# A bilinear tap's corner 3 scaled on ScalarE and added on VectorE in one instruction, with two buffers for its turned values

## The reference

```python
def _L0_conv_ref(x, ...):
    out = relu(frozen_bn(conv2d(x, w1), ...))                 # 1x1, 1024 -> 256
    offset = conv2d(out, w_off, pad=1, bias=b_off)            # 3x3, 256 -> 18
    out = deform_conv3x3(out, offset, w2, pad=1, dil=1)       # 256 -> 256
    out = relu(frozen_bn(out, ...))
    out = frozen_bn(conv2d(out, w3), ...)                     # 1x1, 256 -> 1024
    return relu(out + x)

# inside deform_conv3x3, for each of 9 taps and each pixel, at a position (py, px):
val = (gather(y0, x0) * (wy0 * wx0) + gather(y0, x1) * (wy0 * wx1)
       + gather(y1, x0) * (wy1 * wx0) + gather(y1, x1) * (wy1 * wx1))
return einsum('nckhw,ock->nohw', val, w)

def _L1_conv_ref(x, mask, w1, w2, w3):
    out = relu(_gconv(x * m1, w1, 0)) * m2                    # 4 groups, 1024 -> 256
    out = relu(_gconv(out, w2, 1)) * m2                       # 4 groups, 3x3
    return relu(_gconv(out, w3, 0) + residual)                # 256 -> 1024
```

## Time and profile before

| | |
|---|---|
| median of 3 runs | 2840.26 us (2840.18 to 2841.08) |
| the profiled execution | 2831.85 us |
| its span | 2830.1 us |
| TensorE busy | 2749.0 us, 97% |
| VectorE busy | 2276.2 us, 80% |
| ScalarE busy | 1225.2 us, 43% |
| POOL busy | 1241.1 us, 44% |

### The profile page before, as it was taken

The page is one execution under the profiler, slowest core; times in us unless marked ns, Lnnn a source line. Parts: engine busy times, 40 slices in busy tenths (PEclk is TensorE's granted clock), DMA queues, the critical chain, the costliest instruction groups (busy, mean ns, idle before and its releaser), DMA issues.

```text
span 2830.1 us, 39439 instructions
## 1 busy us (share of the span) xinstructions
PE 2749.0 (97%) x12960; PEld 1518.7 (54%) x12960; DVE 2276.2 (80%) x5216; ACT 1225.2 (43%) x2466; POOL 1241.1 (44%) x1159
## 2 busy tenths in 40 slices
PE   8969999999999999999999999999999999999998
PEld 3435555555555555555555555555555555555552
DVE  2148888888888888888888888888889888888871
ACT  1124444444444444444444444444444444444442
POOL 2046544444444444444444444444444555555530
PEclk9989999999999999999999999999999999999999
DMA  8679988889888899888889988889988888888861
GB/s 328 227 278 343 328 304 303 325 325 333 305 312 298 321 331 328 313 314 303 306 326 325 332 305 309 299 326 327 332 306 295 303 316 317 314 317 318 316 230 77
DMA packets 263691, 864.38 MB, mean 305 GB/s; under 512 B 31810, under 2 KB 72898, under 8 KB 255168
## 3 DMA queue, kind: packets, MB, share of 16 engines
q0 software_dynamic: 165888, 604.05, 60.0%
q1 hardware_dynamic: 79168, 190.68, 18.7%
q10 hardware_dynamic: 18432, 67.12, 6.0%
HBM read 747.72 MB, written 114.02 MB: 304 GB/s over the span
## 4 chain that ended last, share of the span: by engine, by line
PE 93%; DVE 4%; issue 1%; DMA 1%; ACT 1%; SPq 0%; POOL 0%; DVEq 0%; POOLq 0%; ACTq 0%
PE psR L529 15%; PE psA L416 15%; PE psD L509 9%; PE psV L490 9%; PE psD L510 9%; PE psD L511 9%; PE psR L563 9%; PE psR L580 5%; PE psR L542 4%; PE psA L457 3%; PE psR L586 3%; DVE val L947 2%; DVE y L930 1%; PE psD L457 1%; PE psA L437 1%
## 5 line engine op out<-in xcount | busy, mean ns | idle before, releaser
L379 POOL DMA_INDIRECT corners<-corner_tables,samples_in x1152 | 1226.2, 1064 | 1489.1 <-DVE val L947 1056.8
L947 DVE SCALAR_TENSOR_TENSOR val<-corners,samples_in,val 128x256 f32<-128x256 f32 x3456 | 1417.3, 478 | 30.0 <-ACT val L697 24.6
L711 ACT ACTIVATE valT_hi<-psV 128x512 fp32r<-128x512 f32 x576 | 311.6, 593 | 912.8 <-PE psD L511 691.9
L957 DVE TENSOR_TENSOR valT_lo<-psV,valT_hi 128x512 fp32r<-128x512 f32 x576 | 370.5, 685 | 239.0 <-ACT valT_hi L711 222.2
L697 ACT ACTIVATE val<-corners,samples_in 128x256 f32<-128x256 f32 x1152 | 490.4, 503 | 32.9 <-DMA corners<-corner_tables,samples_in 29.1
L509 PE MATMUL psD<-valT_hi,w_hi 128*128 128x512 f32 x1152 | 483.4, 420 | 0.4 <-DVE valT_lo L957 0.4
L529 PE MATMUL psR<-deformed,w_sb 128*128 128x512 f32 x1024 | 463.3, 595 | 2.4 <-ACT y L739 1.9
L510 PE MATMUL psD<-valT_hi,w_lo 128*128 128x512 f32 x1152 | 455.6, 396 | 0.0
L511 PE MATMUL psD<-valT_lo,w_hi 128*128 128x512 f32 x1152 | 454.8, 395 | 0.0
L416 PE MATMUL psA<-x_sb,w_sb 128*128 128x512 f32 x768 | 356.7, 603 | 7.4 <-DMA x_sb<-in_x 7.4
L490 PEld LDWEIGHTS psV<-const_sb,val 128*128 128x128 f32 x2304 | 260.3, 142 | 187.2 <-issue 111.8
(11 more groups left out here) (72 smaller groups left out, 1441.5 us busy)
## 6 DMA issues: line engine op xcount, KB each, us to landing
y<-in_x SPq DMA_DIRECT2D x132, 512.0 KB, 7.8
out<-y ACTq DMA_DIRECT2D x128, 512.0 KB
x_sb<-in_x SPq DMA_DIRECT2D x48, 1024.0 KB
corner_tables<-x_sb SPq DMA_DIRECT2D x128, 256.0 KB
corners<-corner_tables,samples_in POOLq DMA_INDIRECT x1152
y<-in_x SPq DMA_DIRECT2D x7, 2048.0 KB, 9.7
corner_tables<-corners SPq DMA_DIRECT2D x8, 1139.0 KB, 4.2
samples_dram<-samples SPq DMA_DIRECT2D x32, 90.0 KB
```

The costliest lines, as they stand in the source:

```text
L379: nc.gpsimd.indirect_dma_start(corners[:, slot, :], None, table, bass.IndirectOffsetOnAxis(ap=index[:, TAPS * t + k:TAPS * t + k + 1], axi ...
L711: nc.scalar.activation(valT_hi[:, m, :], psV[m][:], ACT.Copy).then_inc(valT_ready, 1)
L947: nc.vector.scalar_tensor_tensor(acc, corners[:, n % GS, corner * CMID:(corner + 1) * CMID], samples_in[:, bpar, w:w + 1], acc, ALU.mult, ...
L957: nc.vector.tensor_tensor(valT_lo[:, m, :], psV[m][:], valT_hi[:, m, :].bitcast(F32), ALU.subtract).then_inc(valT_rest, 1)
```

## The change

ScalarE scales corner 3 as well, in place in `corners`, four instructions a tap ahead of those on corner 0. VectorE then adds corner 3 of all four tiles to `val` in one instruction (`add_products`, L950 after the change) and goes on with corners 1 and 2 (L964). The add waits until all eight scalings of the tap are done, and each instruction for corner 1 waits for the add. A slot of `corners` is free for the next gather after corner 2. `valT_hi` and `valT_lo` have two buffers each, taken in turn, so `valT_copy(k)` waits for tap k-2 and not for tap k-1. The buffer that the runtime keeps for the descriptors of POOL's DMAs is set to 4096 bytes; nothing was set before.

```diff
@@ constants and buffers
+FMA_TAP = 2 * TILES + 1
+N_FMA = TAPS * FMA_TAP
...
-        valT_hi = sb("valT_hi", [P, MC, PIX], F32R)
-        valT_lo = sb("valT_lo", [P, MC, PIX], F32R)
+        valT_hi = sb("valT_hi", [P, 2, MC, PIX], F32R)
+        valT_lo = sb("valT_lo", [P, 2, MC, PIX], F32R)
@@ gpsimd
-                            pool.wait_ge(fma, N_FMA * h + 12 * (last // TILES) + 9 + last % TILES)
+                            pool.wait_ge(fma, N_FMA * h + FMA_TAP * (last // TILES) + TILES + 2 + last % TILES)
@@ tensor, turn_val and tap
-                    pe.wait_ge(fma, N_FMA * h + 12 * (k + 1))
+                    pe.wait_ge(fma, N_FMA * h + FMA_TAP * (k + 1))
...
+                            hi, lo = valT_hi[:, (par + k) % 2, m, :], valT_lo[:, (par + k) % 2, m, :]
@@ scalar, corner0
+                    for tile in range(TILES):
+                        n = TILES * (TAPS * bpar + k) + tile
+                        act.wait_ge(gathered[n % GS], 16 * (n // GS + 1) + 16 * (2 * TILES * TAPS // GS) * (block // 2))
+                        w = (3 * TILES + tile) * TAPS + k
+                        last = corners[:, n % GS, 3 * CMID:]
+                        nc.scalar.activation(last, last, ACT.Copy, scale=samples_in[:, bpar, w:w + 1]
+                                             ).then_inc(first_corner, 1)
                     if not fresh:
                         act.wait_ge(val_turned, 2 * (TAPS * block + k - 1))
@@ scalar, valT_copy
-                    if k >= 1:
-                        act.wait_ge(tap_done, (TAPS - 1) * h + k)
+                    if k >= 2:
+                        act.wait_ge(tap_done, (TAPS - 1) * h + k - 1)
                     elif low > LAG_B:
-                        act.wait_ge(deform_done, 2 * h)
+                        act.wait_ge(deform_done, 2 * h) if k else act.wait_ge(tap_done, (TAPS - 1) * h)
@@ vector
+                def add_products(k):
...
+                    acc = val[:, (bpar + k) % 2]
+                    dve.wait_ge(first_corner, 2 * TILES * (TAPS * block + k + 1))
+                    nc.vector.tensor_tensor(acc, acc, corners[:, slot:slot + TILES, 3 * CMID:], ALU.add
+                                            ).then_inc(fma, 1)
...
-                        if corner == 1:
-                            dve.wait_ge(first_corner, TILES * TAPS * block + TILES * k + tile + 1)
-                        else:
-                            dve.wait_ge(fma, N_FMA * block + 12 * k + 4 * (corner - 2) + tile + 1)
+                        dve.wait_ge(fma, N_FMA * block + FMA_TAP * k + 1 + (tile + 1 if corner == 2 else 0))
...
-                c1, c2, c3 = ({k: [corner(k + 1, c)] for k in range(TAPS)} for c in (1, 2, 3))
+                c1 = {k: [lambda k=k: add_products(k + 1)] for k in range(TAPS)}
+                c2, c3 = ({k: [corner(k + 1, c)] for k in range(TAPS)} for c in (1, 2))
@@ kernel
-    nc = bacc.Bacc("TRN2", target_bir_lowering=False, num_devices=1)
+    nc = bacc.Bacc("TRN2", target_bir_lowering=False, num_devices=1, dynamic_dma_scratch_size=4096)
```

More of the change, by code:

```diff
@@ L507, in tap @@
                             chunk = slice(o * P, (o + 1) * P)
-                            pe.matmul(psD[o][:], w2_hi[:, m, k, chunk], valT_hi[:, m, :], start=first, stop=False)
-                            pe.matmul(psD[o][:], w2_lo[:, m, k, chunk], valT_hi[:, m, :], start=False, stop=False)
-                            mm = pe.matmul(psD[o][:], w2_hi[:, m, k, chunk], valT_lo[:, m, :], start=False, stop=last)
+                            hi, lo = valT_hi[:, (par + k) % 2, m, :], valT_lo[:, (par + k) % 2, m, :]
+                            pe.matmul(psD[o][:], w2_hi[:, m, k, chunk], hi, start=first, stop=False)
+                            pe.matmul(psD[o][:], w2_lo[:, m, k, chunk], hi, start=False, stop=False)
+                            mm = pe.matmul(psD[o][:], w2_hi[:, m, k, chunk], lo, start=False, stop=last)
                             if last:
@@ L694, in corner0 @@
                         n = TILES * (TAPS * bpar + k) + tile
-                        act.wait_ge(gathered[n % GS], 16 * (n // GS + 1) + 16 * (2 * TILES * TAPS // GS) * (block // 2))
                         w = TAPS * tile + k
@@ L704, in valT_copy @@
                         return
[L705 to L706 removed]
+                    if k >= 2:
+                        act.wait_ge(tap_done, (TAPS - 1) * h + k - 1)
                     elif low > LAG_B:
[L708 removed]
+                        act.wait_ge(deform_done, 2 * h) if k else act.wait_ge(tap_done, (TAPS - 1) * h)
                     for m in range(MC):
                         act.wait_ge(val_turned, 2 * (TAPS * h + k) + m + 1)
[L711 removed]
+                        nc.scalar.activation(valT_hi[:, (par + k) % 2, m, :], psV[m][:], ACT.Copy
                                              ).then_inc(valT_ready, 1)
@@ L931, in out_add @@
                                             ).then_inc(out_sum, 1)
+                def add_products(k):
+                    if ("B" if k < TAPS else "next B") not in on:
+                        return
+                    block, bpar = (h, par) if k < TAPS else (h + 1, odd)
+                    k %= TAPS
+                    slot = TILES * (TAPS * bpar + k) % GS
+                    acc = val[:, (bpar + k) % 2]
+                    dve.wait_ge(first_corner, 2 * TILES * (TAPS * block + k + 1))
+                    nc.vector.tensor_tensor(acc, acc, corners[:, slot:slot + TILES, 3 * CMID:], ALU.add
+                                            ).then_inc(fma, 1)
                 def interpolate(k, corner):
@@ L956, in valT_low @@
                         dve.wait_ge(valT_ready, 2 * (TAPS * h + k) + m + 1)
-                        nc.vector.tensor_tensor(valT_lo[:, m, :], psV[m][:],
-                                                valT_hi[:, m, :].bitcast(F32), ALU.subtract
+                        nc.vector.tensor_tensor(valT_lo[:, (par + k) % 2, m, :], psV[m][:],
+                                                valT_hi[:, (par + k) % 2, m, :].bitcast(F32), ALU.subtract
                                                 ).then_inc(valT_rest, 1)
@@ L991, in step @@
                 if low == LAG_B:
-                    for c in range(1, 4):
+                    add_products(0)
+                    for c in (1, 2):
                         interpolate(0, c)
```

1 line of the change is left out of this document (removed).

## The result

The changed kernel takes 2873.18 us (median of 4 runs, 2869.50 to 2874.44) against 2840.22 us before: a ratio of 1.0116, 95% interval 1.0100 to 1.0132. It is slower by 33.0 us, and the whole interval lies above 1; 32.6 us were forecast. The profiled execution took 2874.44 us.

A forecast was written before the change was run, and what follows sets the result against it. TensorE was taken as the bound, so only its idle time counts: +33.6 (short steps), -3 (full steps), +2 (steps 8 and 9) make +32.6 on the 2840.26 median, stated as 2872 us; forecast +20 to +45, range 2832 to 2900.

The forecast's parts named there:

- steps 8 and 9: First two steps that deform: VectorE saves .3 us a tap, but its add waits for all four tiles; +2 us.
- The loop of the short steps: Steps 32 to 39: ScalarE and VectorE wait on each other 9.9 us against TensorE's 7.16; +33.6 us with step ends.
- The full steps: Steps 8 to 31: the longer chain fits by .2 us and turn(1) runs .13 shorter, 23 times; -3 us.
- rival (c): Full steps break too: y_relu(7) comes .5 to 2 us late in 23 steps; 2885 to 2918; with other large losses .17.
- The profiled execution: Profile before took 2831.85 us, 8.4 under the median 2840.26; the forecast sum was added to the median.
- ScalarE's busy time: Over the whole kernel, 1152 more ACTIVATEs at .503 us add 580 us, from 43% to some 64%.
- A sign of being wrong that came: On POOL: the forecast is wrong if gathers (L380) take longer; they took 1.06 us before.
- The price of one scaling: On ScalarE, 128x256 ACTIVATEs stand .40 us apart, .50 for the last, so eight take 3.3; in-place writing might cost more.
- (a): Faster: the loop of ScalarE and VectorE doesn't close, and waits are won; 2815 us; chance .17.
- (b): No change: the longer loop eats just the 1.78 us a short step that it frees; 2840 us; chance .12.

The follow-up runs named there:

- the ring alone: The kernel before with the descriptor ring of POOL's DMAs at 4096 bytes and nothing else: 2840.61 us, ratio 1.0001.
- the second buffers alone: The kernel before with two buffers each for valT_hi and valT_lo and the 4096-byte descriptor ring, nothing else of the change: 2821.92 us, ratio .9932.
- the scalings ahead of y_relu: The changed kernel with ScalarE's eight scalings put before the y_relus for taps 0, 1 and 2 of the short steps: 2839.14 us.
- corner 3 not scaled: The changed kernel without ScalarE's four scalings of corner 3, which is added without its weight: 2824.54 us.
- the kernel without the add: The changed kernel without VectorE's add, so corner 3 is missing from the sum; the wait for eight scalings stays: 2843.96 us.

## Why the prediction was right

The account uses two profiled executions near their medians: that of the ring alone (2840.49 us, the order of before) and that of the changed kernel (2874.44). Marks are the first and the last wait of gconv3 (L580, L582) in the full steps, first in the ring alone, then in the changed kernel, and the end of the last matmul:

```profile
412.39 1.13 PE L580 MATMUL psR<-gb,gw_sb 64*128 64x512 f32 x4 [0.32 <-DVE y L930]
...
2170.98 1.13 PE L580 MATMUL psR<-gb,gw_sb 64*128 64x512 f32 x4 [1.38 <-DVE y L930]
```

```profile
416.90 1.13 PE L582 MATMUL psR<-gb,gw_sb 64*128 64x512 f32 x4 [0.32 <-DVE y L938]
...
2172.93 1.13 PE L582 MATMUL psR<-gb,gw_sb 64*128 64x512 f32 x4 [1.38 <-DVE y L938]
```

The three terms, forecast and measured:

| part | forecast | measured | how |
|---|---|---|---|
| start to the end of step 10 (forecast: steps 8 and 9) | +2 | +4.5 | gconv3's first wait at 416.90 instead of 412.39 |
| the full steps from there | -3 | -2.6 | 1756.0 instead of 1758.6 to its last |
| short steps and tail | +33.6 | +32.1 | 695.7 instead of 663.6 to the end of the last matmul |
| sum | +32.6 | +34.0 | medians: +33.0 |

The sum came out closer than its terms. Too little at the start and too much in the short steps set each other off in part, and that 32.6 and 33.0 lie so near is luck. With the profile of before in the place of the ring alone's the parts are +8.4, -1.0 and +35.1, together 42.5.

*The loop of the short steps* was the step that carried the sum, and its walk held within .1 us at each of the points shown above. Set against the step before, turn_val(5) comes 3.56 us later (39.58 before), where 3.7 to 3.8 were walked. The experiments settle the cause: one order changed on ScalarE gives back 34 us, 1.6 us out of the loop 49 us, 1.25 us out of it 29 us, each against the changed kernel's 2873.2.

*The full steps* fit by .2 us, as walked, so rival (c) did not come; without the second buffers it would have, at 2.7 us a step. The measured term hides that four full steps lasted .55 to .75 longer with waits of turn_val, 1.9 us in all; what delayed them is not settled. In the profile of the ring alone one full step lasted 85.43 instead of 83.74, also unexplained; without it the measured term would be -.9.

*Steps 8 and 9* were mis-sized, +4.5 for +2, inside the bounds of -10.8 to +8. Up to the mark, turn_val's waits were 27.4 us against 24.8 in the profile of the ring alone, the first loads cost .5 more, and TensorE's busy time was 371.8 us at a mean granted clock of .95 against 370.3 at .96. The profiles of before and of the ring alone, with one order of instructions, differ by 3.9 us at this mark (408.47 and 412.39), and there it is the busy time: 366.2 us at a granted clock of .97 against the 370.3. So single profiles don't settle so small a term.

*The profiled execution* of before stood 8.4 us under its median; adding the sum to the median and not to the profile was right: the profiled executions of before and after differ by 42.6 us, the medians by 33.0.

*ScalarE's busy time* rose to 59%, not 64%: the forecast multiplied 1152 by the mean of 503 ns, but neighbours overlap and stand .40 apart, and busy time counts an overlap once; it rose by 456 us. The sum did not use that number.

*A sign of being wrong that came:* the gathers (L380) took POOL longer, 1113 ns on the mean instead of 1064. It didn't mean what the forecast feared. With the same ring the gathers took 1148, 1149 and 1156 ns in the second buffers alone, with the scalings ahead of y_relu and with corner 3 not scaled, and none of these three is slower than the kernel before.

*The price of one scaling.* For 128x256 in float32 the changed kernel shows 503 and 499 ns on ScalarE (L698, L705) and 478 on VectorE (L964), which adds in the same instruction. With the same scalings in another order the loss against the kernel before is gone (2839.14 us).

*The rivals.* (a) needed a loop of 7.16 a tap. The runs suggest a milder rule, that the three turns together decide, for which TensorE needs 21.5 us. From one group of scalings to the next, the changed kernel has 9.83, 8.11 and 6.53 in the step shown (24.5 together), corner 3 not scaled 8.28, 6.51 and 5.24 (20.0, 2824.5 us), and the old interpolation with two buffers 7.36, 5.78 and 5.68 (18.8, 2821.9 us). The last kernel has no wait of conv3 from step 33 on though its first turn is above 7.16, and the prediction's 7.4 for the old loop holds for that first turn alone. (b) needed some 1.2 us a tap less than summed; the kernel without the add has 1.25 less and stands at 2844.0, so that price was right. The fastest version is the old interpolation with two buffers for valT, some .7% faster than before.

## What to carry to other kernels

When work moves from a busy engine to an idle one, add up the loop that the two engines' in-order waits form, from one pass of a wait to the next, and compare it with what the bounding engine needs in that time: here 9.82 us against 7.16 in the first turn. Busy shares don't show it: VectorE's fell from 80% to 75%, and the time rose by 33.0 us. Before, VectorE could start a tap after the first of four scalings and sat idle .55 us ahead of it; now it waits for all eight, and the idle time at the same place of the step is 3.35 us. Merging four instructions into one made that change silently. What the merging costs here by itself isn't shown: no run splits the add by tile again, so that each part waits for its own scalings alone. And take a change of two halves apart, in both directions: here the buffers alone won 18.7 us and the interpolation on top of them gave 51 away, while the interpolation without them costs 124.

## What the runs showed of the hardware

An ACTIVATE that writes over its own source costs what one into another buffer costs: 503 ns (L698) and 499 ns (L705) for 128x256 float32. POOL's gathers ran at a mean of 1064 ns both before and with the small ring alone, and at 1020 to 1156 ns in the six other kernels, which have the small ring too; so their pace moves with something other than the ring, and what that is, is not shown.
